# The expert stage's loop with 24 tiles in its body, run twice, in place of 8 tiles run six times

## What is computed

```python
    probs = jax.nn.softmax(flat @ gate_w + gate_b, axis=-1)
    top_p, top_i = jax.lax.top_k(probs, 2)
    top_w = top_p / (jnp.sum(top_p, axis=-1, keepdims=True) + 1e-09)
    comb = jnp.zeros((T, E)).at[rows, top_i].add(top_w)
    for e in range(8):
        h = jax.nn.gelu(flat @ w1[e] + b1[e], approximate=False)      # 256 -> 1024
        out = out + comb[:, e:e + 1] * (h @ w2[e] + b2[e])            # 1024 -> 256
```

## Time and profile before

| | us |
|---|---|
| median of 3 runs | 729.14 (729.09 to 731.33) |
| the profiled execution | 731.6 |
| its span in the trace | 729.9 |
| PE busy in the span | 608.2 (83%) |
| DVE busy | 465.5 (64%) |
| ACT busy | 318.1 (44%) |
| POOL busy | 213.2 (29%) |

### The profile page before, as it was taken

The page is one execution under the profiler, slowest core; times in us unless marked ns, Lnnn a source line. Parts: engine busy times, 40 slices in busy tenths (PEclk is TensorE's granted clock), DMA queues, the critical chain, the costliest instruction groups (busy, mean ns, idle before and its releaser), DMA issues.

```text
span 729.9 us, 14331 instructions
## 1 busy us (share of the span) xinstructions
PE 608.2 (83%) x3834; PEld 535.4 (73%) x3835; DVE 465.5 (64%) x1556; ACT 318.1 (44%) x626; POOL 213.2 (29%) x193
## 2 busy tenths in 40 slices
PE   6652589989888985148999999999999999999982
PEld 3541477767777974037998898899899899899872
DVE  1788699898989885614565564564565555555650
ACT  1645577867676642013333343333334333333330
POOL 5230121212746666711122122122221221221221
PEclk9887699999999996559999999999999999999995
DMA  9380887868786972411255372744626528322211
GB/s 280 127 329 16 314 305 274 315 238 306 272 314 217 356 297 80 134 53 32 45 153 189 55 284 44 245 97 105 231 44 165 181 37 280 65 38 45 31 15 14
DMA packets 50487, 120.82 MB, mean 166 GB/s; under 512 B 7564, under 2 KB 39184, under 8 KB 44304
## 3 DMA queue, kind: packets, MB, share of 16 engines
q1 hardware_dynamic: 30128, 98.07, 37.2%
q0 software_dynamic: 11136, 14.00, 11.5%
q10 hardware_dynamic: 9184, 8.28, 4.2%
HBM read 68.22 MB, written 52.11 MB: 165 GB/s over the span
## 4 chain that ended last, share of the span: by engine, by line
PE 58%; DVE 23%; issue 7%; ACT 5%; POOL 2%; DVEq 1%; DMA 1%; ACTq 0%; SPq 0%; POOLq 0%
PE ps L843 42%; PE ps L870 6%; DVE wset L1114 4%; DVE stt L1023 2%; POOL rows_by_expert L440 2%; PE ps L674 2%; PE ps L836 2%; PE ps L741 2%; PE ps L730 1%; DVE img L1108 1%; ACT xh L540 1%; DVE tc L1014 1%; PE ps L778 1%; ACT img L534 1%; DVE bst L993 1%
## 5 line engine op out<-in xcount | busy, mean ns | idle before, releaser
L462 POOL DMA_INDIRECT out<-ys,xr x56 | 86.7, 1548 | 318.8 <-DVE ys L1393 248.0
L843 PE MATMUL ps<-wset,hTh 128*128 x896 | 163.6, 283 | 7.1 <-DVE hTl L1361 7.0
L843 PEld LDWEIGHTS ps<-wset,hTh 128*128 128x128 f32 x896 | 141.8, 190 | 15.0 <-issue 11.0
L843 PE MATMUL ps<-wset,xrTh 128*128 x448 | 147.5, 411 | 0.0
L635 ACT ACTIVATE hb<-hb 128x512 f32<-128x512 f32 x112 | 70.5, 632 | 140.6 <-DVE hb L1382 140.6
L843 PE MATMUL ps<-wset,hTl 128*128 x448 | 126.4, 282 | 0.0
L641 ACT CAST hTh<-ps 128x512 fp32r<-128x512 f32 x112 | 60.1, 589 | 102.0 <-PE ps L870 101.6
L1388 DVE TENSOR_TENSOR yb<-ps,bset 128x256 f32<-128x256 f32 x56 | 23.8, 425 | 124.2 <-PE ps L843 124.2
L843 PEld LDWEIGHTS ps<-wset,xrTh 128*128 128x128 f32 x448 | 81.2, 191 | 15.6
L843 PE MATMUL ps<-wset,xrTl 128*128 x224 | 89.5, 400 | 0.0
L1382 DVE TENSOR_TENSOR hb<-ps,bset 128x512 f32<-128x512 f32 x112 | 76.0, 685 | 17.2 <-PE ps L843 17.2
(11 more groups left out here) (181 smaller groups left out, 943.9 us busy)
## 6 DMA issues: line engine op xcount, KB each, us to landing
split_weights<-wset SPq DMA_DIRECT2D x16, 2048.0 KB, 7.4
wset<-split_weights SPq DMA_DIRECT2D x32, 1024.0 KB, 7.2
wset<-in_ew SPq DMA_DIRECT2D x16, 1024.0 KB, 10.2
xr<-rows_by_expert ACTq DMA_DIRECT2D x56, 132.5 KB, 2.1
bset<-in_eb SPq DMA_DIRECT2D x8, 640.0 KB, 8.9
img<-in_x SPq DMA_DIRECT2D x8, 392.0 KB, 6.4
out<-img SPq DMA_DIRECT2D x16, 196.0 KB
rows_by_expert<-rows,slot POOLq DMA_INDIRECT x64, 3.4
```

Of the source, the lines that this page charges most:

```text
L462: pool.indirect_dma_start(out, bass.IndirectOffsetOnAxis(xr[:, r % XR, C + E:ROW].bitcast(U32), 0), ys[:, r % YS, :], None, compute_op=ALU ...
L843: last = pe.matmul(dst, rows_k[:, k * 128:(k + 1) * 128], wset[:, bass.ds(column(k) + rest, width)], start=(k == 0 and n == 0), stop=(k == ...
```

## The change

A constant `TURN = 24` is new, and the loops of the four engines hold 24 turns in their bodies and are run twice. The reading of the packed word moves: it is done at every fourth turn of the body, ahead of that turn, and no longer twice at the top. The waits' values are the same for each tile. So the branch back is taken once on each engine in place of five times; the words that are read stay one for each four turns.

```diff
+TURN = 24
...
-            with pool.Fori(0, SLOTS // 8 - 1) as g:
-                for r in range(8):
-                    add_rows(8 * g + 4 + r, r + 4)
+            with pool.Fori(0, (SLOTS - 8) // TURN) as g:
+                for r in range(TURN):
+                    add_rows(TURN * g + 4 + r, r + 4)
...
-            with act.Fori(0, SLOTS // 8 - 1) as g:
-                for r in range(8):
-                    act_slot(8 * g + 4 + r, r + 4)
+            with act.Fori(0, (SLOTS - 8) // TURN) as g:
+                for r in range(TURN):
+                    act_slot(TURN * g + 4 + r, r + 4)
...
-            with pe.Fori(0, SLOTS // 8 - 1) as g:
-
-                of = experts_of(2 * g + 1), experts_of(2 * g + 2)
-                for q in range(8):
-                    mine = of[q // 4]
-                    pe_slot(8 * g + 4 + q, (q + 4) % XR, mine[q % 4], mine[q % 4 + 1], g * 16 + (q // 4) * 16 + 16)
+            with pe.Fori(0, (SLOTS - 8) // TURN) as g:
+
+                for q in range(TURN):
+                    if q % 4 == 0:
+                        mine = experts_of(TURN // 4 * g + q // 4 + 1)
+                    pe_slot(TURN * g + 4 + q, (q + 4) % XR, mine[q % 4], mine[q % 4 + 1],
+                            g * (TURN // XR * 16) + (q + 4) // XR * 16 + 16)
```

More of the change, by code:

```diff
@@ L1426, in _ @@
                 vec_slot(m, m % XR)
[L1427 to L1433, removed]
+            with dve.Fori(0, (SLOTS - 8) // TURN) as g:
+                for q in range(TURN):
+                    if q % 4 == 0:
+                        mine = experts_of(TURN // 4 * g + q // 4 + 1)
+                    vec_slot(TURN * g + 4 + q, (q + 4) % XR, mine[q % 4], mine[q % 4 + 1], mine[q % 4 + 2],
+                             g * (TURN // XR * 16) + (q + 4) // XR * 16 + 16)
             of = experts_of(SLOTS // 4 - 1)
```

## The result

The changed kernel takes 734.79 us (median of 7 runs, 732.72 to 736.27) against 730.3 us for the kernel before (7 runs, the three on record among them, 729.09 to 731.64): a ratio of 1.006, 95% interval 1.0046 to 1.0074. It is slower by 0.6%, 4.4 us. The forecast was 728.0 us, 1.1 us faster.

The account below looks back on a forecast made before the run. The prediction took PE to bound the kernel inside a loop body. Its terms, -7.4 + 3.3 - 0.5 + 3.5 = -1.1 us, took 729.1 to a forecast of 728.0 us, with a range of 725.0 to 731.5.

Parts of the forecast that it names:

- What goes, -7.4 us for five returns: At the loop's branch back on all engines: five returns of 1.48 us each vanish, -7.4 us.
- The mechanism of the 1.48 us: At each old return: PE's sequencer runs dry for 0.26 us, and DVE's branch and two word reads delay `hTl`.
- The reads inside the bodies, +3.3 us: Ten new places inside the loop bodies where a word is read, 0.33 us each: +3.3 us (1.0 to 4.5).
- The entry, -0.5: At loop entry, one read replaces two and PE's 0.66 us gap goes: -0.5 us (0 to -0.7).
- The fetch at the return: At the one return left, the first instruction block must be fetched, 3.0 us a fetch; the return costs +3.5 us.
- the third rival: Two instruction fetches in a row at the remaining return, +1.9 to +4.5 us, 731.0 to 733.6 us; chance 0.22.
- That DVE's fetch decides, not PE's: At the remaining return both fetches run side by side; DVE's gives the larger cost, 3.5 us against 2.5 for PE's only.
- its far end (9.1 us, +4.5): Return's upper bound: two fetches of 4.3 us one after the other plus 0.5, 9.1 us; total +4.5, 733.6 us.
- The marks named in advance: Signs: PE idle over 1 us near 503 us, about 12 queue-8 packets per pass, every fourth turn 7.0-7.1 us, entry gap gone.
- Idle time over 5 us: PE's idle time at the remaining return; over 5 us would show the forecast wrong and point to the third rival.

## Why the prediction was wrong

- **What goes, -7.4 us for five returns: right.** With 48 turns and no return all but the entry's part of the gain of 7.7 us is this term.
- **The mechanism of the 1.48 us: right on DVE.** PE's own gap was a share in name only; with PE's reads spread and DVE's not, a return still costs 1.49.
- **The reads inside the bodies, +3.3 us: right in kind, too large.** They cost 2.0 (0.2 each, within the bounds 0.1 to 0.45). The turn behind the loop was the nearest row, but its branch matters: 2.42 us from `h_turn` to `hTl` cost 0.33, 2.35 us cost 0.2, and some 2.12 us cost nothing in nine turns of ten.
- **The entry, -0.5: -0.7.** The turn behind it stayed as it was.
- **The fetch at the return: the cause was right, and this is the step that failed, on size.** The sum had +3.5 us; the return costs 10.5. Three things were wrong in the term. A fetch was priced at 3.0 us between DMAs that took 2.1 and 4.3; the stall ahead of `h_turn` is 4.41 us on top of the sequencer's lead, so the real price is about 5; at DVE's own branch 5.33 us were seen. The nearest rows didn't ask whether the DMA engines were taken at that moment, and they were (1.00). There were two fetches in a row and not one, which stood as the third rival with 0.22, at 731.0 to 733.6; aligning the top took 4.3 us off the return. And neither the sum nor any rival had the clock: it was 0.50 from 508 to 518 us, worth 2.8 us.
- **That DVE's fetch decides, not PE's: wrong.** PE alone gives 9.1 of the 10.5; that of the others, 7.2 alone, lies beside it.
- **The range** ended at 731.5, inside the third rival's own 731.0 to 733.6 and below what two fetches and a slow clock give. The term that no row of before could price should have kept its far end (9.1 us, +4.5) in the range. That the measured +4.4 us equals this far end is in part luck: the return cost 1.4 us more than 9.1, and the reads 1.3 less than their term. The kernel before also came out at 730.3 and not 729.14; from 729.14 the same loss would still give 733.5.
- **The marks named in advance.** The place (near 503 us), 12 packets in the first pass and 14 in the second, the entry's gap gone: all seen. Every fourth turn took 6.89 to 7.04 us, a little less than the 7.0 to 7.1 named, and PE's waits list none for `hTl`. "Idle time over 5 us" was named as the sign of rival 3, and it is 7.2.

## What to carry to other kernels

A longer loop body removes returns, but once it exceeds what the engine keeps of its instructions each return cost 6 to 11 us here in place of 1.5 or less; either stay well under that size or have no return at all. Look at the instruction queues of the DMA by stretch: no packets in later passes means that the body is kept, and that is a property to preserve. What a return and register reads cost depends on where in the turn they stand: on an engine that waits 2 us for another in each turn, the loop's end belongs into that wait.

## What the runs showed of the hardware

- Queue 8 carries PE's instructions in packets of 16 KB (0.20 MB by 12) and queue 14 the others' in packets of 8 KB (0.13 MB by 16). PE reuses a body of 64 KB and doesn't reuse one of 128 KB.
- A return whose target isn't kept stalled PE for 3.0 to 4.4 us beyond its lead; a second stall of 1.9 to 4.8 us followed after one transpose, and didn't with the top at the start of its block. Straight code, up to 48 turns (24 packets on queue 8), ran with no stall.
- Where PE stood still at a return the granted clock went from 1.00 to 0.50, and it was still 0.51 over the 6.0 us in which PE was busy again (512.20 to 518.20 in the changed kernel); this cost 2.8 us. It fell to 0.50 as well behind the stall of 2.73 us at the end of the hinted loop.
- A hint for the closing branch removes the stall where the branch is taken and leaves one where the loop ends.
